# A graph network layer: edge weights computed turned, biased in ScalarE's copy, and turned back by TensorE

## What is computed

```python
# layer 0
h   = norm(x)
x  += segment_sum(h[src], dst) @ W_rel.T + b_rel + h @ W_root.T
# layer 1
h   = norm(x)
ew  = silu(edge_features @ We1 + be1) @ We2 + be2      # one weight vector per edge
agg = segment_sum(h[src] * ew, dst)
x  += h + silu(agg @ Wn1 + bn1) @ Wn2 + bn2
```

## Time and profile before

| | |
|---|---|
| Median of 3 runs | 4800.75 us (4791.8 to 4805.88) |
| The profiled execution | 4849.66 us, span 4847.9 us |
| TensorE's granted clock, mean | 0.665 of full speed |
| Busy in the span | PE 50%, PEld 38%, DVE 26%, ACT 10%, POOL 61% |
| DMA | 296.77 MB, mean 61 GB/s |

### The profile page before, as it was taken

The page is one execution under the profiler, slowest core; times in us unless marked ns, Lnnn a source line. Parts: engine busy times, 40 slices in busy tenths (PEclk is TensorE's granted clock), DMA queues, the critical chain, the costliest instruction groups (busy, mean ns, idle before and its releaser), DMA issues.

```text
span 4847.9 us, 35780 instructions
## 1 busy us (share of the span) xinstructions
PE 2418.4 (50%) x10938; PEld 1841.8 (38%) x10938; DVE 1276.0 (26%) x2181; ACT 479.4 (10%) x842; POOL 2970.8 (61%) x3135
## 2 busy tenths in 40 slices
PE   1332323232323232322447677777666777767667
PEld 0322322232222222222334445555454555544545
DVE  2511111111111111111323333333333333333334
ACT  3400000000000000000101111111111111111111
POOL 5366666666666666666465656666656666656662
PEclk9755556555656565655667767777767777767777
DMA  5222222222221222222222222222222222222222
GB/s 135 61 53 52 55 53 56 54 53 53 56 54 51 56 55 54 51 56 55 62 59 61 65 62 64 65 69 64 65 61 64 65 67 66 64 61 64 64 63 59
DMA packets 230579, 296.77 MB, mean 61 GB/s; under 512 B 68580, under 2 KB 160278, under 8 KB 230433
## 3 DMA queue, kind: packets, MB, share of 16 engines
q0 software_dynamic: 100096, 205.20, 16.8%
q10 hardware_dynamic: 61378, 60.59, 4.6%
q1 hardware_dynamic: 69086, 30.79, 2.4%
HBM read 269.87 MB, written 26.48 MB: 61 GB/s over the span
## 4 chain that ended last, share of the span: by engine, by line
another core or an unknown queue 44%; PE 26%; issue 17%; DVE 10%; DVEq 2%; ACT 1%; POOL 0%; DMA 0%; ACTq 0%; SPq 0%; POOLq 0%
PE seg_a L370 7%; PE seg_b L370 5%; PE ew_a L416 4%; PE ew_b L416 3%; DVE onehot L711 3%; PE hid_b L410 3%; PE hid_a L410 2%; DVE ew_a L817 2%; DVE rows L825 2%; DVE ew_b L817 1%; DVEq L719 1%; PE node L430 0%; DVE e_stats L625 0%; PE node L381 0%
## 5 line engine op out<-in xcount | busy, mean ns | idle before, releaser
L320 POOL DMA_INDIRECT rows<-h_rows,idx x3060 | 2905.5, 950 | 1783.2 <-issue 952.2
L370 PE MATMUL seg_a<-onehot,rows 128*128 128x128 f32 x3312 | 662.9, 358 | 1136.9 <-DVE onehot L711 445.2
L370 PEld LDWEIGHTS seg_a<-onehot,rows 128*128 128x128 f32 x3312 | 601.9, 268 | 1221.4 <-issue 934.2
L370 PE MATMUL seg_b<-onehot,rows 128*128 128x128 f32 x2944 | 572.5, 340 | 809.3 <-issue 576.9
L370 PEld LDWEIGHTS seg_b<-onehot,rows 128*128 128x128 f32 x2944 | 504.8, 249 | 855.7 <-issue 659.9
L711 DVE TENSOR_TENSOR onehot<-iota_ps,dst_rel 128x1536 f32<-128x1536 f32 (+1 forms) x278 | 461.3, 1659 | 1.0 <-DVE dst_rel L699 0.6
L817 DVE TENSOR_TENSOR ew_a<-ew_a,be_all 128x512 f32<-128x512 f32 x207 | 144.6, 699 | 1044.7 <-remote 703.2
L416 PE MATMUL ew_b<-we_sb,hidden 128*128 128x128 f32 x1472 | 289.3, 357 | 224.6 <-ACT hidden L578 177.1
L416 PEld LDWEIGHTS ew_b<-we_sb,hidden 128*128 128x128 f32 x1472 | 245.2, 252 | 406.5 <-ACT hidden L578 210.3
L416 PEld LDWEIGHTS ew_a<-we_sb,hidden 128*128 128x128 f32 x1664 | 268.6, 245 | 246.3 <-issue 169.0
L416 PE MATMUL ew_a<-we_sb,hidden 128*128 128x128 f32 x1664 | 310.8, 345 | 81.4 <-ACT hidden L578 55.2
(11 more groups left out here) (122 smaller groups left out, 1148.4 us busy)
## 6 DMA issues: line engine op xcount, KB each, us to landing
rows<-h_rows,idx POOLq DMA_INDIRECT x3060
ef_a<-ef_blocks ACTq DMA_DIRECT2D x70, 300.0 KB
node_work<-ef_blocks ACTq DMA_DIRECT2D x47, 300.0 KB
xs<-x SPq DMA_DIRECT2D x40, 256.0 KB
ys<-y_rows SPq DMA_DIRECT2D x26, 256.0 KB
out<-xs ACTq DMA_DIRECT2D x26, 256.0 KB
y_rows<-ys ACTq DMA_DIRECT2D x25, 256.0 KB
h_rows<-node_work ACTq DMA_DIRECT2D x23, 256.0 KB
```

The costliest lines, as they stand in the source:

```text
L320: pool.indirect_dma_start(out=rows[:, u, t, :], out_offset=None, in_=table, in_offset=bass.IndirectOffsetOnAxis(ap=idx[:, j:j + 1], axis=0 ...
L370: mm = pe.matmul(seg[g % 2][:, 0:P], rows[:, u, t, :], onehot[:, g % 2, k * TB + t, :], start=(k == 0 and t == 0), stop=(last and t == TB ...
```

## The change

Layer 1's edge weights are made with We2 stationary and the 512 hidden columns of a block streamed: one product, whose result is turned (feature by edge) and overwrites the block's hidden bank, now one of three. ACT copies it to SBUF and adds be2, which is now one value per partition. Four TensorE transposes turn it back into `ew_ps`. DVE's `edge_bias` and its semaphore go; `message` reads `ew_ps`. The segment sum of a block moves one step back in TensorE's order, and ACT runs one SiLU ahead. The bank of `iota_ps` becomes the third hidden bank, and the one-hot compare, in both layers, reads the iota from SBUF. The copies lie in `agg[0]`, the table of layer 0.

```diff
-        iota_ps = bank("iota_ps")
-        hid_ps, ew_ps = [bank("hid_a"), bank("hid_b")], [bank("ew_a"), bank("ew_b")]
+        hid_ps = [bank("hid_a"), bank("hid_b"), bank("hid_c")]
+        ew_ps = [bank("ew_a"), bank("ew_b")]
+        weights = agg[0][:, 0:2 * BLOCK].rearrange("p (b e) -> p b e", e=BLOCK)
...
-            def edge_hidden(i, u):
+            def edge_hidden(i, u, freed):
                 g, k = u // GB, u % GB
+                if freed is not None:
+                    hold(pe, s_weights, freed + 1)
...
             def edge_weights(i, u):
                 pe.wait_ge(s_silu, i * U + (u + 1))
+                pe.matmul(hid_ps[u % 3][:, :], we2_sb[:, :], hidden[:, u % 2, :], start=True, stop=True
+                          ).then_inc(s_ew_t, 1)
+
+            def edge_turned(i, u):
+                pe.wait_ge(s_weights, i * U + (u + 2))
                 for t in range(TB):
-                    mm = pe.matmul(ew_ps[u % 2][:, t * D:(t + 1) * D], hidden[:, u % 2, t * P:(t + 1) * P],
-                                   we2_sb[:, :], start=True, stop=True)
-                mm.then_inc(s_ew, 1)
+                    tr = pe.transpose(ew_ps[u % 2][:, t * P:(t + 1) * P], weights[:, u % 2, t * P:(t + 1) * P],
+                                      ident[:, :])
+                tr.then_inc(s_ew, 1)
...
                         if u + 2 < U:
-                            edge_hidden(i, u + 2)
+                            edge_hidden(i, u + 2, i * U + u)
                             edge_weights(i, u + 1)
+                            edge_turned(i, u)
...
-                        pe.wait_ge(s_msg, i * U + (u + 1))
-                        segment_sum(1, u)
-                        if u + 1 == U:
                             edge_weights(i + 1, 0)
+                        if u > 0:
+                            summed_block(u - 1)
+                    summed_block(U - 1)
...
+            def edge_weights(i, u):
+                act.wait_ge(s_ew_t, i * U + (u + 1))
+                nc.scalar.activation(weights[:, u % 2, :], hid_ps[u % 3][:, :], ACT.Identity,
+                                     bias=be2_col[:, :]).then_inc(s_weights, 1)
...
-                        edge_silu(i, u)
                         g = u // GB
                         if u == blocks_of(g)[-1]:
                             load_ef(it + (g + 2) // G, (g + 2) % G)
+                        if u + 1 < U:
+                            edge_silu(i, u + 1)
+                        else:
+                            edge_silu(i + 1, 0)
+                        edge_weights(i, u)
...
-                    iota_ps[:, 0:P].unsqueeze(1).to_broadcast([P, tiles, P]),
+                    iota_f[:, :].unsqueeze(1).to_broadcast([P, tiles, P]),
...
-            def edge_bias(i, u):
-                dve.wait_ge(s_ew, i * U + (u + 1))
-                ew = ew_ps[u % 2][:, :].rearrange("p (t f) -> p t f", t=TB)
-                v.tensor_tensor(ew, ew, be2_all[:, :].unsqueeze(1).to_broadcast([P, TB, D]),
-                                ALU.add).then_inc(s_add, 1)
...
             def message(i, u):
-                dve.wait_ge(s_add, i * U + (u + 1))
+                dve.wait_ge(s_ew, i * U + (u + 1))
```

More of the change, by code:

```diff
@@ L120, in build @@
         hidden = sb("hidden", [P, 2, BLOCK])
-        iota_ps = bank("iota_ps")
         seg = [bank("seg_a"), bank("seg_b")]
-        hid_ps, ew_ps = [bank("hid_a"), bank("hid_b")], [bank("ew_a"), bank("ew_b")]
+        hid_ps = [bank("hid_a"), bank("hid_b"), bank("hid_c")]
+        ew_ps = [bank("ew_a"), bank("ew_b")]
         node = bank("node")
-        node_t, node_o = [node, hid_ps[0], ew_ps[0]], [node, *seg]
+        node_t, node_o = [node, hid_ps[0], ew_ps[0]], [node, hid_ps[1], ew_ps[1]]
+        weights = agg[0][:, 0:2 * BLOCK].rearrange("p (b e) -> p b e", e=BLOCK)
         h_table = agg[1]
@@ L131, in build @@
                  *(s.rearrange("p (t f) -> p t f", t=TB) for s in (hT[0], aggT[0]))]
-        h_turn = [*hid_ps, *ew_ps, seg[0]]
+        h_turn = [*hid_ps, *ew_ps]
         assert LATE <= 3
@@ L236, in _ @@
             for dst, w in ((w_rel_sb, w_rel_t), (w_root_sb, w_root_t), (we1_sb, we1), (we2_sb, we2),
-                           (wn1_sb, wn1), (wn2_sb, wn2), (be1_col, be1), (bn1_col, bn1)):
+                           (wn1_sb, wn1), (wn2_sb, wn2), (be1_col, be1), (be2_col, be2), (bn1_col, bn1)):
                 sp.dma_start(dst[:, :], w).then_inc(s_wts, 16)
-            for dst, b in ((b_rel_all, b_rel), (be2_all, be2), (bn2_all, bn2)):
+            for dst, b in ((b_rel_all, b_rel), (bn2_all, bn2)):
                 sp.dma_start(dst[:, :], b.to_broadcast([P, D])).then_inc(s_wts, 16)
@@ L347, in _ @@
             pe.sem_inc(s_seg[1], G)
+            pe.sem_inc(s_weights, 1)
             for r in range(H_SETS):
@@ L404, in _ @@
                 side_by_side([node_update0(passes * (ITERS - 1) + j * LATE + r, r) for r in range(LATE)])
-            def edge_hidden(i, u):
+            def edge_hidden(i, u, freed):
                 g, k = u // GB, u % GB
+                if freed is not None:
+                    hold(pe, s_weights, freed + 1)
                 if k == 0:
                     pe.wait_ge(s_ef[g % 2], i * (8 * G) + 16 * (g // 2 + 1))
-                pe.matmul(hid_ps[u % 2][:, :], we1_sb[:, :], ef[g % 2][:, k, :], start=True, stop=True
+                pe.matmul(hid_ps[u % 3][:, :], we1_sb[:, :], ef[g % 2][:, k, :], start=True, stop=True
                           ).then_inc(s_hid, 1)
@@ L433, in node_update1 @@
                 return {4: hidden_layer, 7: product}
-            edge_hidden(0, 0)
-            edge_hidden(0, 1)
+            edge_hidden(0, 0, None)
+            edge_hidden(0, 1, None)
             edge_weights(0, 0)
@@ L441, in _, with summed_block @@
                     steps = node_update1(loop_group(it), i, 0, i * G + 1)
+                    def summed_block(u):
+                        pe.wait_ge(s_msg, i * U + (u + 1))
+                        segment_sum(1, u)
                     for u in range(U):
@@ L445, in _ @@
                         if u + 2 < U:
-                            edge_hidden(i, u + 2)
+                            edge_hidden(i, u + 2, i * U + u)
                             edge_weights(i, u + 1)
+                            edge_turned(i, u)
                         elif u + 1 < U:
                             edge_weights(i, u + 1)
-                            edge_hidden(i + 1, u + 2 - U)
-                        else:
-                            edge_hidden(i + 1, u + 2 - U)
-                        pe.wait_ge(s_msg, i * U + (u + 1))
-                        segment_sum(1, u)
-                        if u + 1 == U:
+                            edge_hidden(i + 1, 0, i * U + (u + 1))
+                            edge_turned(i, u)
+                        else:
+                            edge_hidden(i + 1, 1, i * U + (u + 1))
+                            edge_turned(i, u)
                             edge_weights(i + 1, 0)
+                        if u > 0:
+                            summed_block(u - 1)
+                    summed_block(U - 1)
+            hold(pe, s_weights, passes * ITERS * U + 2)
             hold(pe, s_silu, passes * ITERS * U + 2)
@@ L577, in edge_silu @@
                 act.wait_ge(s_hid, i * U + (u + 1))
-                nc.scalar.activation(hidden[:, u % 2, :], hid_ps[u % 2][:, :], ACT.Silu,
+                nc.scalar.activation(hidden[:, u % 2, :], hid_ps[u % 3][:, :], ACT.Silu,
                                      bias=be1_col[:, :]).then_inc(s_silu, 1)
+            def edge_weights(i, u):
+                act.wait_ge(s_ew_t, i * U + (u + 1))
+                nc.scalar.activation(weights[:, u % 2, :], hid_ps[u % 3][:, :], ACT.Identity,
+                                     bias=be2_col[:, :]).then_inc(s_weights, 1)
             load_ef(0, 0)
             load_ef(0, 1)
+            edge_silu(0, 0)
             with act.Fori(0, passes) as p:
@@ L591, in _ @@
                             load_ef(it + (g + 2) // G, (g + 2) % G)
+                        if u + 1 < U:
[3 more added lines that the diff above has]
+                        edge_weights(i, u)
                         if u in steps:
                             steps[u]()
-            edge_silu(passes * ITERS, 0)
             edge_silu(passes * ITERS, 1)
-            hold(act, s_ew, passes * ITERS * U + 1)
+            edge_weights(passes * ITERS, 0)
+            hold(act, s_ew, passes * ITERS * U)
             for b in range(2):
@@ L839, in edge_blocks @@
                 steps = node_update1(i, 0, i + 1)
-                edge_bias(i, 0)
                 for u in range(U):
```

14 lines of the change are left out of this document (6 added, 8 removed).

## The result

| | before | after |
|---|---|---|
| Median of 4 runs | 4802.34 us (4791.8 to 4805.88) | 4887.41 us (4861.67 to 4904.35) |
| After to before | | 1.0164, 95% interval 1.0131 to 1.0197 |
| The profiled execution | 4849.66 us, span 4847.9 | 4861.67 us, span 4859.9 |

A forecast was written before the change was run, and what follows sets the result against it. POOL's waits for late TensorE signals were taken as the bound; +74 (21 iterations x 3.5), +11 tail and +1 start made +86 us, +1.8%, giving 4886. The forecast's own range was 4840 to 4940, the whole range 4680 to 5010.

The forecast's parts named there:

- What bounds the kernel: Layer 1: POOL's waits for TensorE signals held until gathers drain; 68 gathers x 1.25 = 85.0 of 105.2 us per iteration.
- The one-hot's iota from SBUF: One-hot compare on DVE: reading the iota from SBUF changes it by -0.03 to +0.15 us, hidden there.
- The rival that named it: Both layers: the one-hot holds POOL up to 1.75 us, six times per iteration, up to +460 us; chance 0.02.
- The sign named for that rival: POOL's gathers: starts more than 1.25 us apart over a one-hot would show that the one-hot holds POOL.
- One short wait turns into a long one: POOL, layer 1: one of four short waits per iteration turns long, +3.5 us, +74 over 21 iterations; chance 0.38.
- Its sum for a window: TensorE, layer 1: with the added work of three blocks, 16.5 to 18.4 of 18.1 us busy, fitting barely.
- TensorE's +0.6 us per block: Layer 1: product and turning take 1.50 instead of 0.89 us per block at the upper clock.
- ACT's extra pass: ACT, layer 1: one more 512-column pass from PSUM, 0.69 us per block, 2.1 us per three blocks, hidden.
- DVE's bias: DVE, layer 1: dropping it takes 0.7 us from the long wait's chain once per iteration.
- The tail: After the last gather, TensorE is the bound: 14 blocks at about 0.8 us more, +11 us.
- Clock and tables: Two rivals: TensorE's lower clock stays, 5030 us, chance 0.07; ACT loads two tables per block, +100 us or more, 0.02.

The follow-up runs named there:

- a1: The change, run again beside before on a quick chip: 4221.04 us, ratio 1.0546.
- a3: The change with the one-hot's iota back in PSUM and two hidden banks, on a quick chip: 4001.82 us, ratio 0.9993.
- h1: Before, with POOL waiting within each group of layer 1 until the gathers so far have landed, on a quick chip: 4273.13 us.
- g1: The change with layer 0's one-hot reading a copy of the iota in the third hidden bank, on a quick chip: 4088.22 us, ratio 1.0215.
- e1: Before with only the one-hot's iota moved to SBUF, both layers, on a waiting chip: 4903.58 us, ratio 1.0149.
- e2: The change with the iota back in PSUM, so two hidden banks, on a waiting chip: 4972.18 us, ratio 1.0273.
- n2: The change without layer 1's gathers, their index loads and DVE's wait for them, on a quick chip: 3568.68 us.
- n1: Before without layer 1's gathers, their index loads and DVE's wait for them, on a quick chip: 3373.07 us.
- e3: Before without DVE's edge bias and its semaphore (be2 not added), on a waiting chip: 4811.14 us, ratio 0.9956.
- e2s: The change with two hidden banks and the iota in SBUF, on a waiting chip: ratio 1.0344.
- a2: Before with only the one-hot's iota moved to SBUF, both layers, on a quick chip: 4225.83 us, ratio 1.0559.

## Why a one-hot holds a gather, and why the row of before hid it

From the traces, all pairs of one DVE operation with two SBUF inputs and one gather that overlap, by how long after the DVE operation the gather starts (counted from the single instructions; no view gives it). Of after, 34 pairs from 0 to 0.1 us and above 1.2 us are left out, and 7 whose gather an earlier one-hot already held.

```
DVE operation            gather starts     pairs  gather takes    gather ends
after, L739 one-hot      before it           176  0.94 (normal)
after, L739 one-hot      0.1 to 0.5 later    106  2.14 mean       0.82 after the one-hot
after, L739 one-hot      0.5 to 0.8 later     57  1.88 mean       0.82 after the one-hot
after, L739 one-hot      0.8 to 1.2 later     68  1.44 mean       0.82 after the one-hot
before, L765             0.01 to 0.02 later   20  0.946 (normal)  L765 takes 733 ns, not 683
```

The rows show a lock. A gather that starts while DVE reads two SBUF tiles ends 0.82 us after DVE has finished, wherever in the operation it started; its first 0.13 us (0.95 - 0.82) pass, then it stands still. In a1's layer 0, on the other kind of chip, the one-hot ends at 1001.63 and the gather at 1002.45, 0.82 later again:

```profile
1000.41 1.22 DVE L739 TENSOR_TENSOR onehot<-iota_f,dst_rel 128x1024 f32<-128x1024 f32 x1
1000.67 1.78 POOL L322 DMA_INDIRECT rows<-h_rows,idx  x1 [0.30 <-issue]
```

With the iota in PSUM the same pair of operations, in a3, leaves the gather at its 0.94:

```profile
997.20 1.75 DVE L742 TENSOR_TENSOR onehot<-iota_ps,dst_rel 128x1536 f32<-128x1536 f32 x1
997.55 0.94 POOL L323 DMA_INDIRECT rows<-h_rows,idx  x1 [0.30 <-issue]
```

A gather that has started before DVE, or at most 0.03 us after it, goes through. At 0 to 0.03 us DVE is the one to wait: such one-hots take 1.79 to 1.82 instead of 1.748 us. The L765 of the earlier trace rows meets a gather 21 times, and 20 times of these at just this offset, 0.01 to 0.02 us; the 21st gather started 0.37 us before it, and L765 took 683 ns. The row from which I took the price was real, and it was the one phase in which the price falls on the other engine.

The same operation in other phases confirms it. h1's layer 0 is that of before, on a quick chip; there the operation (now L769) meets 20 gathers that start 0.24 to 0.58 us after it, and 18 of them take more than 1.1 us, while the operation itself takes its 0.68 us. This one starts 0.34 us in and ends 0.82 after it:

```profile
529.87 0.68 DVE L769 TENSOR_TENSOR ys<-xs,node_work 128x512 f32<-128x512 f32 x1
530.21 1.16 POOL L320 DMA_INDIRECT rows<-h_rows,idx  x1 [0.30 <-issue]
```

So the contention was in the kernel before as well, and only the phase on the waiting chip hid it. The small long gathers of g1's layer 0 are these too.

The size follows. With gathers 1.25 us apart, the first to start in a one-hot of 1.75 us starts x later, x anywhere from 0 to 1.25, and takes 1.75 - x + 0.82 instead of 0.95: 1.0 us more on average. For the one-hot of two blocks (1.22 us) it is 1.09 - x where that is positive, 0.5 on average. Per iteration that makes 5 x 1.0 + 0.5 = 5.5; layer 0 on the quick chip measured 91.0 - 85.2 = 5.8. In layer 1 it is 3.8: there most of a1's gathers that meet a one-hot, 109 of 141, start 0.8 us or more after it and are held for less.

The Trainium skill (SBUF — State Buffer, section on who interferes with whom) has the rule, a VectorE instruction with two SBUF inputs against a GpSimd instruction that reads SBUF, and says besides that issue order decides who blocks. The traces agree with both: the gather that comes second is held over the operation's end, the DVE operation that comes second for some 50 ns.

## Why the prediction was right and wrong, step by step

- **What bounds the kernel**: right for the kind of chip of the first runs, and of that kind alone. 68 x 1.25 = 85.0 us of issue per iteration was exact: it is what is left on the quick chip (85.05 in a3's layer 1). The reading that TensorE's signals arrive late in a bunch stands as seen; its cause stays open.
- **"The one-hot's iota from SBUF"**, priced at -0.03 to +0.15 us, hidden on DVE: this is the step that failed. On DVE it was right (1.748 us in both). On POOL, where the sum had nothing, it is 1.0 us per one-hot. The rival that named it got a chance of 0.02, on the word of a single row in a single phase. Half of its upper bound, 230 of 460 us, was near for the gathers: they are 231 us longer in after and 212 (3124.0 - 2911.5) on the quick chip. There all of it reaches the end; on a waiting one 70 of 208 did (e1). The sign named for that rival, gathers more than 1.25 us apart over a one-hot, is what after shows (2.43 us), in a run whose time fits the forecast.
- **"One short wait turns into a long one"**, +3.5 us x 21 = +74: did not happen. 20 long waits against 19, an iteration of 105.9 us, not 108 to 110. With one hidden bank fewer there are 32 long waits and 110.9 us (e2), but there TensorE waits for a bank; that its added work alone makes a window fail, no run shows. The prediction gave the third bank no weight. Its sum for a window was also not "barely" within it: the upper end, 18.4 us, is more than 18.1.
- **TensorE's +0.6 us per block** at the upper clock: too high. From start to start, product and turning take 0.96 + 0.44 = 1.40 us in n2 (2402.93 to 2404.33), not 1.50. What they replace takes 1.00 us in n1 (2401.10 to 2402.10); the 0.89 of the prediction ended at the next weight load, which starts 0.11 us earlier. That is +0.4, and by busy time a block costs only 4.4 / 17 = 0.26 more. In n2:

```profile
2402.93 1.12 PE L419 MATMUL hid_c<-hidden,we_sb 128*128 128x512 f32 x2
...
2403.89 0.60 PE L425 MATMUL ew_b<-ident,agg 128*128 128x128 f32 x4
...
2404.33 0.39 PE L372 MATMUL seg_a<-onehot,rows 128*128 128x128 f32 x2
```

In n1:

```profile
2401.10 1.16 PE L415 MATMUL ew_b<-we_sb,hidden 128*128 128x128 f32 x8
...
2401.99 0.97 PEld L369 LDWEIGHTS seg_a<-onehot,rows 128*128 128x128 f32 x8
2402.10 1.06 PE L369 MATMUL seg_a<-onehot,rows 128*128 128x128 f32 x8
```

- **ACT's extra pass** hidden: right (a3 at 0.9993 has it). **DVE's bias**: 0.7 per iteration predicted, 1.0 measured in e3 (0.5 to 1.5).
- **The tail**, +11: not seen. It takes 56.8 us after the last gather, where before took 71.6, but e1 and e3, in the old order, took 72.0 and 59.6, and e2 and e2s, in the new one, 73.8 and 75.8, so one trace says nothing of it. On the quick chip it is 19.0, 22.2 and 19.3 in a1, a2 and a3.
- **Clock and tables**: neither rival played a part. The granted clock of layer 1 did not fall, it is 0.77 from 3000 to 4500 us of after (third number from the end below), where before has 0.71. The table loads, forecast to stay at one per iteration, fell from 23 to the one of this row. Its 28 us of ACT are hidden either way:

```profile
3000.00:4500.00 1500.00, 1053.50 (x4050) 598.50 (x4050) 344.10 (x443) 332.62 (x501) 996.85 (x978) 0.77 0.24 65
```

```profile
L597 ACT ACT_TABLE_LOAD x1 | 1.3, 1283 | 6.5 <-issue 6.5
```

What isn't settled: on a waiting chip the turned order with three banks and no contention was not run. The ratios of the change and of e1, 1.0164 and 1.0149, leave some 0.15% for it, with about half a per cent of uncertainty to each side, from different chips. So that the turning is free on such a chip too isn't shown, only that the iota is enough for the whole loss.

## What to carry to other kernels

Before a VectorE operand moves from PSUM to SBUF, count the operation's SBUF inputs: with two of them it stops GpSimd's gathers, and the cost is to be looked for on GpSimd, not on VectorE. A row that speaks against contention has to be looked at for its phase: where the two operations always start at the same offset, it is one sample, however often it is repeated. And a number that was met is no proof of its sum; here changing one operand alone (e1, a2) and undoing it (a3) showed that the sum was another.

## What the runs showed of the hardware

- The same program has medians of 4800 to 4833 us on some chips and of 4002 to 4004 on others. The gathers are alike (0.95 busy, 1.25 apart); on the waiting ones the signals of TensorE reach the other engines late while gathers run, 8.3 us in the timeline of after. I know no reason.
- A gather that starts 0.04 us or more into a VectorE operation with two SBUF inputs, but before its last 0.13 us, is held and ends 0.82 us after it, on either kind of chip, for the one-hot (1.75 us) and, on a quick one, for a plain addition (0.68 us, h1).
- What slack is worth differs by chip: 212 us of longer gathers cost 213 us where POOL never waits; where it does, 208 us cost 70 (e1), and 230 cost some 34, uncertain by as much (e2s against e2).
